# A table of due slots for side work in a three-phase attention kernel: the second phase's normalisation and post block put earlier, and more room ahead of a few steps

## Chip, cores and metric

One core of a Trainium2 chip runs the whole program. The metric is the device time of one execution in microseconds. The kernel is written in Bass with the order on every engine fixed when the program is built, and each engine works through its own list in order.

## What is computed

The input `x` has 32 sequences of 56 tokens with 160 features; `ctx_768` has 1500 context rows of 96 features for each sequence. Four blocks follow one another:

- L0: three short attentions (16 tokens each) against parts of the context, a weighted sum, output projection and residual.
- L1: layer norm, self attention (20 heads of 64), then cross attention over all 1500 context rows, then a gated feed-forward.
- L2: cross attention over 1496 context rows with 8 heads of 20, plus a small two-step attention over the 4 last context rows.
- L3: like L1 with 20 heads of 8.

Cut to its core, a long cross attention is:

```python
q = layer_norm(x) @ wq          # per head
scores = q @ (ctx @ wk).T * scale
out = softmax(scores) @ (ctx @ wv)
x = out @ wo + bo + x
```

## The kernel before

**Phases and pairs.** The program has three phases: phase 0 does L0 and L1, phase 1 (the "second phase" here) does L2, phase 2 does L3. A phase takes the 32 sequences as 16 pairs. For each pair and each half `b` of it (one sequence) the function `main` on TensorE runs the long cross attention: the context is cut into 12 chunks of 125 rows, and the heads into groups of at most 8 (8, 8 and 4 heads in phases 0 and 2; one group of 8 in phase 1). One chunk and group is a tile. It takes three matmuls into `ps_s` for the scores (L1133 to L1135), two exponentials on ScalarE (L1825 to `p32`, L1827 to `p_hi`), a subtraction on GpSimd (L1614, `p_lo`) and three matmuls into `ps_u` for the output (L1148 to L1150), three tiles behind the scores. "A group" below means three matmuls of one such set, 448 columns wide.

**Slots.** `main` counts slots: tile n has its scores at slot 2n and the outputs of tile n-3 at slot 2n+1. So one half is 24 slots long in phase 1, and 72 in phases 0 and 2.

**Side work.** Everything else is woven between the slots: `pre` (the short attentions and norms of the next pair), `context` (transposing the context, L1058, L1783, L1432), `queries` (L695 into `ps_c`, L1760, L1762, L1410), `maxima` (matmuls L1076 and the reductions L1455 and L1458 on VectorE, then `mneg` L1463, a transpose L1081 and `q_hi` L1468, without which the next half's scores can't begin), `post` (the projection L1094 of the attention's result, and in phases 0 and 2 the feed-forward), `hand` (L1495). Each is a generator that yields step numbers. The table `PARTS` gives for each part and phase a tuple (number of steps, weight, {step: extra room ahead of it}); `lane` lays a list of parts over the slots of one half, from `start` to the half's length less `tail`, and scales them to fit; `weave` runs main's slots and the lanes in order of slot. Room in `PARTS` is therefore relative: what one step gets is taken from the others of its lane. The same function runs on every engine.

**Normalisation.** At the end of a half, ScalarE copies the result out of `ps_u` into `uT` (L1815, at slot 6 of the next half in phase 1). Row 96 of it holds the sums. SyncE stores them (L623), loads them spread over partitions into `srec` (L626), VectorE takes the reciprocal (L1479) at slot `RECIP`, SyncE stores them (L629) and loads them broadcast to all partitions (L639, into `w_area` in phases 1 and 2), and VectorE multiplies `uT` by them (L1485) at slot `POST - 1`. `post` may start at slot `POST` in phase 1; it waits for that product. VectorE's list is strictly in order: while the reciprocal or the product waits for its transfer, the maxima behind it wait too.

```python
RECIP = 13
POST = 20
...
if t.ph == 1:
    weave(main(t, 0, first=first), lane(parts), lane(end, POST), *norm)
```

In phase 1, `parts` are `split`, `context(t, 1)` and `maxima(t, 1)`, and `end` is `post` of the pair before, `hand`, and the first 9 steps of `pre` of the next pair. In phase 1 these first steps are: take x (L1195 `x_mid`, L742, L745), the csT copy (L1334), L923 and L926, `pT` (L1338), L933, the masked keys `kvb` (L1340, L1260, L1344), the short scores L941, their maximum and difference (L1223, L1225), the exponential (L1651) and L763. So they are a chain between TensorE, VectorE and ScalarE.

## Time and profile before

| | us |
|---|---|
| median of 3 executions (lowest, highest) | 5963.16 (5962.99, 5965.48) |
| the profiled execution's own time | 5963.19 |
| span in the profile, first to last instruction | 5961.4 |
| TensorE matmul busy | 5579.6 (94%) |
| TensorE weight load busy | 4580.3 (77%) |
| VectorE, ScalarE, GpSimd busy | 2818.5, 3101.7, 3095.7 |
| mean granted TensorE clock | 0.961 of full |

The table's last line is the share of the full clock that was granted to TensorE over the span; windows of the trace give it stretch by stretch. TensorE's idle time comes with the instruction that ended it. All waits quoted are in microseconds unless marked ns.

### The profile page before, as it was taken

How to read it: one execution, taken by the hardware profiler on the slowest of the kernel's cores; microseconds unless marked ns; L12 is line 12 of the kernel's file. 1: busy time of each engine (PE TensorE's matmuls, PEld its weight loads, DVE VectorE, ACT ScalarE, POOL GpSimd, SP SyncE). 2: the span in 40 equal slices, each digit the busy share in tenths (PEclk: the TensorE clock that was granted, in tenths of full speed). 3: DMA queues.
4: the chain of work that ended last, by engine and by line, in shares of the span. 5: the costliest groups of instructions: out<-in, count | busy, mean ns of one | idle time of the engine just before them, and what ended most of it. 6: DMA issues, size and time to landing. Idle time of an engine off the chain costs nothing.

```text
span 5961.4 us, 92283 instructions
## 1 busy us (share of the span) xinstructions
PE 5579.6 (94%) x34224; PEld 4580.3 (77%) x34224; DVE 2818.5 (47%) x5171; ACT 3101.7 (52%) x7280; POOL 3095.7 (52%) x3472
## 2 busy tenths in 40 slices
PE   7999999999999999998989999799999999999998
PEld 5777777777777777786767767578888888888887
DVE  2444444444444444443555555255445455545452
ACT  1455555555554555553544544356566656566655
POOL 0445454444544445462555545256666666666665
PEclk8899999999999999997999989689999999999999
DMA  2000000000000000000111111100000000000000
GB/s 56 13 17 17 14 17 17 17 16 17 17 10 17 12 17 17 17 21 15 31 29 29 31 26 29 25 17 24 17 17 20 17 21 20 20 17 20 17 21 12
DMA packets 85964, 119.97 MB, mean 20 GB/s; under 512 B 42814, under 2 KB 65194, under 8 KB 85514
## 3 DMA queue, kind: packets, MB, share of 16 engines
q1 hardware_dynamic: 85514, 114.07, 6.9%
q8 instruction: 271, 4.44, 0.3%
q14 instruction: 179, 1.47, 0.1%
HBM read 109.56 MB, written 4.46 MB: 19 GB/s over the span
## 4 chain that ended last, share of the span: by engine, by line
PE 64%; DVE 18%; ACT 9%; DMA 3%; POOL 3%; issue 3%; ACTq 0%; POOLq 0%; SPq 0%; DVEq 0%
PE ps_c L695 13%; DVE mpiece L1458 8%; PE ps_s L1133 6%; PE ps_s L1134 5%; PE ps_s L1135 5%; PE ps_u L1148 5%; PE ps_c L1076 5%; PE ps_u L1150 4%; PE ps_u L1149 4%; PE ps_c L1094 3%; ACT p_hi L1827 2%; ACT p L1825 2%; POOL p_lo L1614 2%; DVE ctx_hi L1449 2%; DVE uT L1485 2%
## 5 line engine op out<-in xcount | busy, mean ns | idle before, releaser
L1614 POOL TENSOR_TENSOR p_lo<-p,p_hi 125x448 fp32r<-125x448 f32 (+2 forms) x2688 | 2716.5, 1019 | 2320.8 <-ACT p_hi L1827 1652.9
L1825 ACT ACTIVATE p<-ps_s 125x448 f32<-125x448 f32 (+2 forms) x2688 | 1324.7, 493 | 1822.6 <-PE ps_s L1135 1617.5
L1827 ACT ACTIVATE p_hi<-ps_s 125x448 fp32r<-125x448 f32 (+2 forms) x2688 | 1319.1, 491 | 0.0
L1458 DVE TENSOR_REDUCE mpiece<-ps_c 125x1 f32<-125x500 f32 (+1 forms) x1984 | 1226.8, 666 | 92.9 <-PE ps_c L1076 89.8
L1133 PE MATMUL ps_s<-q_hi,ctxT_hi 105*125 105x448 f32 (+3 forms) x2688 | 1005.0, 374 | 51.6 <-DVE q_hi L1468 28.5
L1148 PE MATMUL ps_u<-p_hi,ctx_hi 125*97 125x448 f32 (+2 forms) x2688 | 961.6, 358 | 16.1 <-ACT uT L1815 15.1
L1134 PE MATMUL ps_s<-q_lo,ctxT_hi 96*125 96x448 f32 (+2 forms) x2688 | 926.0, 345 | 0.0
L1135 PE MATMUL ps_s<-q_hi,ctxT_lo 96*125 96x448 f32 (+2 forms) x2688 | 922.0, 343 | 0.0
L1149 PE MATMUL ps_u<-p_hi,ctx_lo 125*96 125x448 f32 (+2 forms) x2688 | 914.7, 340 | 0.0
L1150 PE MATMUL ps_u<-p_lo,ctx_hi 125*97 125x448 f32 (+2 forms) x2688 | 913.8, 340 | 0.0
L1076 PE MATMUL ps_c<-ctxT_hi,q_hi 96*125 96x500 f32 (+1 forms) x2112 | 845.3, 425 | 67.5 <-DVE mpiece L1458 58.5
L1133 PEld LDWEIGHTS ps_s<-q_hi,ctxT_hi 105*125 105x125 f32 (+2 forms) x2688 | 507.1, 189 | 201.9 <-ACT p_hi L1827 55.3
L1076 PEld LDWEIGHTS ps_c<-ctxT_hi,q_hi 96*125 96x125 f32 (+1 forms) x2112 | 394.6, 188 | 254.5 <-DVE mpiece L1458 183.3
L1134 PEld LDWEIGHTS ps_s<-q_lo,ctxT_hi 96*125 96x125 f32 (+1 forms) x2688 | 513.1, 191 | 47.7
L1135 PEld LDWEIGHTS ps_s<-q_hi,ctxT_lo 96*125 96x125 f32 (+1 forms) x2688 | 513.0, 191 | 35.9
L1149 PEld LDWEIGHTS ps_u<-p_hi,ctx_lo 125*96 125x96 f32 (+1 forms) x2688 | 444.3, 165 | 91.7
L1150 PEld LDWEIGHTS ps_u<-p_lo,ctx_hi 125*97 125x97 f32 (+1 forms) x2688 | 440.3, 164 | 83.1
L1148 PEld LDWEIGHTS ps_u<-p_hi,ctx_hi 125*97 125x97 f32 (+1 forms) x2688 | 443.2, 165 | 59.6 <-issue 23.7
L1593 POOL TENSOR_TENSOR ctx_lo<-ctx_raw,ctx_hi 125x192 fp32r<-125x192 f32 x576 | 330.1, 582 | 184.7 <-DVE ctx_hi L1449 184.7
L695 PE MATMUL ps_c<-hT,w_m 80*96 80x112 f32 x3072 | 329.0, 268 | 33.1 <-ACT hT L1644 30.3
L695 PEld LDWEIGHTS ps_c<-hT,w_m 80*96 80x96 f32 x3072 | 318.3, 170 | 51.0 <-issue 43.7
L1410 DVE TENSOR_TENSOR q_lo<-ps_c,q_hi 96x224 fp32r<-96x224 f32 x192 | 74.4, 388 | 475.1 <-ACT q_hi L1762 475.1
(226 smaller groups left out, 5898.4 us busy)
## 6 DMA issues: line engine op xcount, KB each, us to landing
ctx_raw<-in_ctx SPq DMA_DIRECT2D x96, 562.5 KB
pT<-recs SPq DMA_DIRECT2D x32, 490.0 KB, 3.6
w_area<-recs SPq DMA_DIRECT2D x32, 490.0 KB, 3.6
w_area<-recs SPq DMA_DIRECT2D x32, 196.0 KB, 3.9
cs<-in_ctx SPq DMA_DIRECT2D x192, 6.0 KB, 3.2
x_between<-x_out SPq DMA_DIRECT2D x32, 80.0 KB
x_in<-x_between SPq DMA_DIRECT2D x32, 80.0 KB
w_area<-in_L_xattn_wq SPq DMA_DIRECT2D x2, 800.0 KB, 6.0
```

The costliest lines, as they stand in the source:

```text
L695: z = mm(dst, lhsT(i), rhs(i), start=(first and i == 0), stop=(last and i == 1))
L1076: mm(C(0, wide, n % banks(t), 0, PIECE), q_hi[0:DC, b, wide * k:wide * k + wide], ctxT_hi[0:DC, b, PIECE * r:PIECE * r + PIECE], start=Tru ...
L1133: mm(dst, ctxT_hi[0:rows_, b, k], q_hi[0:rows_, b, q], start=True, stop=False)
L1134: mm(dst, ctxT_hi[0:DC, b, k], q_lo[:, b, q], start=False, stop=False)
L1135: mm(dst, ctxT_lo[:, b, k], q_hi[0:DC, b, q], start=False, stop=True).then_inc(*sig("sc_psum"))
L1148: mm(dst, ctx_hi[0:kp, cb, c, :], p_hi[0:kp, k % RING, 0:w], start=(c == 0), stop=False)
L1149: mm(ps_u[0:DC, g, 0:w], ctx_lo[0:kp, cb, c, :], p_hi[0:kp, k % RING, 0:w], start=False, stop=False)
L1150: mm(dst, ctx_hi[0:kp, cb, c, :], p_lo[0:kp, k % 3, 0:w], start=False, stop=(c == NC - 1)).then_inc(*sig("pv_done"))
L1458: z = V.tensor_reduce(mpiece[0:wide, k, r:r + 1], C(0, wide, n % banks(t), 0, PIECE), AX.X, ALU.max)
L1614: P.tensor_tensor(p_lo[0:kp, k % 3, 0:w], p32[0:kp, k % 2, 0:w], p_hi[0:kp, k % RING, 0:w].bitcast(F32), ALU.subtract).then_inc(*sig("pl_r ...
L1825: A(p32[0:kp, k % 2, 0:w], ps_s[0:kp, k % 2, 0:w], ACT.Exp, scale=DH[t.ph] ** -0.5)
L1827: A(p_hi[0:kp, k % RING, 0:w], ps_s[0:kp, k % 2, 0:w], ACT.Exp, scale=DH[t.ph] ** -0.5)\
```

## The change

Numbers alone change in the table: nine entries of extra room grow (in `pre` steps 8, 27, 30, 35 of phase 0, step 5 of phase 1 and step 7 of phase 2; `queries` step 1 in phases 0 and 2; `post` step 6 in phase 0). For phase 1, `RECIP` goes from 13 to 10 and `POST` from 20 to 16, the lane with the maxima of the first half ends three slots earlier, and phase 2's first `pre` starts at slot 20 of phase 1's last half, before at 26 (behind the last score).

```diff
-            "pre": ((40, 3, {4: 1, 7: 0.5, 8: 3, 10: 1.5, 14: 1.5, 16: 3, 18: 2, 22: 2, 27: 2.5, 30: 1.5, 34: 1, 35: 0.5, 37: 1,
-                             38: 1.5, 39: 2, 40: 4.5}), (29, 3.5, {5: 2, 15: 1.5, 22: 0.5, 23: 2}), (20, 2.5, {2: 3, 6: 1.5, 7: 0.5, 9: 2, 11: 0.5, 13: 1, 15: 1, 19: 2, 20: 1})),
-            "queries": ((7, 1, {1: 2, 7: 3}), (3, 3, {1: 1}), (7, 1, {1: 2, 7: 2})),
+            "pre": ((40, 3, {4: 1, 7: 0.5, 8: 4, 10: 1.5, 14: 1.5, 16: 3, 18: 2, 22: 2, 27: 3, 30: 2, 34: 1, 35: 1.5, 37: 1,
+                             38: 1.5, 39: 2, 40: 4.5}), (29, 3.5, {5: 2.5, 15: 1.5, 22: 0.5, 23: 2}), (20, 2.5, {2: 3, 6: 1.5, 7: 1.2, 9: 2, 11: 0.5, 13: 1, 15: 1, 19: 2, 20: 1})),
+            "queries": ((7, 1, {1: 5, 7: 3}), (3, 3, {1: 1}), (7, 1, {1: 5, 7: 2})),
...
-            "post": ((15, 3, {1: 1, 6: 1, 14: 1}), (2, 1.5, {1: 1}), (15, 3, {1: 0.5, 6: 1.5})),
+            "post": ((15, 3, {1: 1, 6: 2, 14: 1}), (2, 1.5, {1: 1}), (15, 3, {1: 0.5, 6: 1.5})),
...
-        RECIP = 13
-        POST = 20
+        RECIP = (13, 10, 13)
+        POST = (20, 16, 20)
...
-                    weave(main(t, 0, first=first), lane(parts), lane(end, POST), *norm)
+                    weave(main(t, 0, first=first), lane(parts, 0.0, TAIL - 1), lane(end, POST[1]), *norm)
...
-                    lanes = [lane([part("pre", side.pre, At(t.ph + 1, 0, ahead=True))], POST + 6.0)]
+                    lanes = [lane([part("pre", side.pre, At(t.ph + 1, 0, ahead=True))], POST[t.ph] + (4.0 if t.ph else 6.0))]
```

(`normalise` reads `RECIP[t.ph]` and `POST[t.ph]` now.)

How this moves instructions is seen at two places of a steady pair of phase 1. First VectorE in the pair's first half, from the last context piece to the product: before,

```order
L1458 TENSOR_REDUCE mpiece<-ps_c 112x1
L1449 CAST ctx_hi<-ctx_raw 125x4x96
L1458 TENSOR_REDUCE mpiece<-ps_c 112x1
L1455 TENSOR_REDUCE mpiece<-ps_c 112x1
L1479 RECIPROCAL srec<-srec 112x4
L1449 CAST ctx_hi<-ctx_raw 125x4x96
L1458 TENSOR_REDUCE mpiece<-ps_c 112x1 x2
L1449 CAST ctx_hi<-ctx_raw 125x4x96
L1455 TENSOR_REDUCE mpiece<-ps_c 112x1
L1458 TENSOR_REDUCE mpiece<-ps_c 112x1 x2
L1455 TENSOR_REDUCE mpiece<-ps_c 112x1
L1485 TENSOR_TENSOR uT<-uT,w_area 97x8x56
```

and now:

```order
L1479 RECIPROCAL srec<-srec 112x4
L1458 TENSOR_REDUCE mpiece<-ps_c 112x1
L1449 CAST ctx_hi<-ctx_raw 125x4x96
L1458 TENSOR_REDUCE mpiece<-ps_c 112x1
L1455 TENSOR_REDUCE mpiece<-ps_c 112x1
L1449 CAST ctx_hi<-ctx_raw 125x4x96
L1458 TENSOR_REDUCE mpiece<-ps_c 112x1 x2
L1449 CAST ctx_hi<-ctx_raw 125x4x96
L1455 TENSOR_REDUCE mpiece<-ps_c 112x1
L1458 TENSOR_REDUCE mpiece<-ps_c 112x1
L1485 TENSOR_TENSOR uT<-uT,w_area 97x8x56
```

The reciprocal now stands ahead of the first reduction instead of behind the third, and the product behind the seventh of the twelve instead of behind the ninth.

Second TensorE near the end of the same half, from L933 to the short scores L941 and the transposed maxima L1081: before,

```order
L933 MATMUL ps_u<-pT,w_s 80x128 x2
L1133 MATMUL ps_s<-q_hi,ctxT_hi 124x448
L1134 MATMUL ps_s<-q_lo,ctxT_hi 124x448
L1135 MATMUL ps_s<-q_hi,ctxT_lo 124x448
L1148 MATMUL ps_u<-p_hi,ctx_hi 97x448
L1149 MATMUL ps_u<-p_hi,ctx_lo 96x448
L1150 MATMUL ps_u<-p_lo,ctx_hi 97x448
L941 MATMUL ps_u<-kvb,qo 64x256 x4
L1081 MATMUL ps_c<-ident,mneg 4x112
```

and now:

```order
L933 MATMUL ps_u<-pT,w_s 80x128 x2
L1133 MATMUL ps_s<-q_hi,ctxT_hi 124x448
L1134 MATMUL ps_s<-q_lo,ctxT_hi 124x448
L1135 MATMUL ps_s<-q_hi,ctxT_lo 124x448
L1081 MATMUL ps_c<-ident,mneg 4x112
L1148 MATMUL ps_u<-p_hi,ctx_hi 97x448
L1149 MATMUL ps_u<-p_hi,ctx_lo 96x448
L1150 MATMUL ps_u<-p_lo,ctx_hi 97x448
L1133 MATMUL ps_s<-q_hi,ctxT_hi 124x448
L1134 MATMUL ps_s<-q_lo,ctxT_hi 124x448
L1135 MATMUL ps_s<-q_hi,ctxT_lo 124x448
L941 MATMUL ps_u<-kvb,qo 64x256 x4
```

The transposed maxima come ahead of the short scores, and one group more stands in front of the latter. Over the whole stretch from L1094 to L763 TensorE had four groups woven in before and has eight now; the four that were added stood ahead of L1094 before. In phases 0 and 2 single groups change places with a side step: in phase 0 one group now stands ahead of L763, one ahead of the queries' L695, and L1094 comes one group earlier while L1101 stays; in phase 2 one more group stands ahead of the queries' L695, and ScalarE has the `hT` it waits for (L1644) one pair of exponentials earlier.

## Rows read from the trace of the kernel before

**Rows 1.** The page, busy time: us (share of the span), instructions.

```profile
PE 5579.6 (94%) x34224; PEld 4580.3 (77%) x34224; DVE 2818.5 (47%) x5171; ACT 3101.7 (52%) x7280; POOL 3095.7 (52%) x3472
```

**Rows 2.** Windows: length, busy PE PEld DVE ACT POOL, PEclk, DMA, GB/s.

```profile
2794.00:3683.40 889.40, 814.80 (x4595) 624.90 (x4592) 500.50 (x996) 443.56 (x980) 485.64 (x506) 0.93 0.13 29
...
3049.20:3109.50 60.30, 54.73 (x329) 42.05 (x328) 36.02 (x71) 31.63 (x70) 34.65 (x36) 1.00 0.13 28
...
3235.30:3300.10 64.80, 59.89 (x328) 45.94 (x328) 35.35 (x72) 31.72 (x70) 34.41 (x36) 0.89 0.11 29
3365.60:3426.60 61.00, 55.91 (x328) 43.32 (x328) 35.08 (x71) 31.61 (x70) 34.43 (x36) 0.97 0.13 28
...
219.10:2469.40 2250.30, 2144.91 (x13812) 1775.57 (x13813) 1022.73 (x1821) 1162.01 (x2710) 1105.17 (x1264) 1.00 0.05 16
3945.20:5744.60 1799.40, 1746.79 (x11154) 1482.43 (x11153) 919.79 (x1667) 1087.51 (x2607) 1119.03 (x1262) 1.00 0.06 19
```

**Rows 3.** Windows, phase 1: a pair's time at half clock.

```profile
3175.80:3189.50 13.70, 12.05 (x53) 8.95 (x54) 3.71 (x8) 4.07 (x8) 3.07 (x3) 0.50 0.01 2
```

**Rows 4.** Timeline, PE, one pair (start, length, instruction, [idle before it, ended by]).

```profile
3106.38 2.44 PE L1094 MATMUL ps_u<-w_n,uT 96*128 96x160 f32 x16 [0.47 <-DVE uT L1485]
...
3114.84 1.09 PE L941 MATMUL ps_u<-kvb,qo 80*64 80x256 f32 x8 [0.74 <-DVE kvb L1344]
...
3117.96 0.73 PE L1133 MATMUL ps_s<-q_hi,ctxT_hi 100*125 100x448 f32 x1 [1.75 <-DVE q_hi L1468]
...
3119.24 1.05 PE L763 MATMUL ps_c<-ident,sm 128*128 128x128 f32 x4
```

**Rows 5.** Timeline, DVE and ACT, the same pair.

```profile
3097.18 0.68 DVE L1458 TENSOR_REDUCE mpiece<-ps_c 112x1 f32<-112x500 f32 x1 [0.78 <-PE ps_c L1076]
...
3104.73 1.59 DVE L1485 TENSOR_TENSOR uT<-uT,w_area 97x448 f32<-97x448 f32 x1 [0.41 <-DMA w_area<-recs]
...
3111.68 0.28 DVE L1338 COPY pT<-ps_u 4x128 f32<-4x128 f32 x1 [0.50 <-PE ps_c L926]
...
3114.61 0.15 DVE L1463 TENSOR_REDUCE mneg<-mpiece 112x4 f32<-112x12 f32 x1
...
3117.28 0.58 ACT L1651 ACTIVATE sm<-sm 128x448 f32<-128x448 f32 x1 [2.78 <-DVE sm L1225]
```

**Rows 6.** Timeline, SyncE's queue, the same pair; then DMA issues, phase 1, to landing.

```profile
3095.39 0.32 SPq L626 DMA_DIRECT2D srec<-sums  x1
3099.42 0.31 SPq L629 DMA_DIRECT2D recs<-srec  x1
3100.81 0.30 SPq L639 DMA_DIRECT2D w_area<-recs  x1
...
w_area<-recs SPq DMA_DIRECT2D x25, 196.0 KB, 3.9
...
srec<-sums SPq DMA_DIRECT2D x25, 1.8 KB, 1.6
```

**Rows 7.** PE's waits, phase 0, 14 pairs (total, times, longest).

```profile
PE ps_c L1076 <- DVE mpiece L1458: 28.4, 44, 1.0
PE ps_c L695 <- ACT hT L1644: 13.1, 14, 0.9
PE ps_c L763 <- DVE sm L1241: 12.9, 13, 1.0
PE ps_c L1101 <- DVE xn L1521: 9.6, 14, 0.7
```

**Rows 8.** PE's waits, phase 2, 14 pairs.

```profile
PE ps_c L695 <- ACT hT L1644: 14.5, 15, 1.0
```

**Rows 9.** Timeline, PE, the end of phase 1's last half.

```profile
3765.86 0.36 PE L1148 MATMUL ps_u<-p_hi,ctx_hi 124*97 124x448 f32 x1
...
3766.47 0.36 PE L1148 MATMUL ps_u<-p_hi,ctx_hi 124*97 124x448 f32 x1
...
3771.06 0.62 PE L755 MATMUL ps_c<-ident,xn 128*80 128x128 f32 x2 [3.82 <-DVE xn L1216]
```

More of the change, by code:

```diff
@@ L1476, in normalise @@
                     tiles = t.heads // 2
-                    yield RECIP
+                    yield RECIP[t.ph]
                     dve.wait_ge(*got("su_loaded", t, 16 * (b + 1)))
@@ L1480, in normalise @@
                     for g, (h0, n) in enumerate(t.groups):
-                        yield POST - 1 + (APART[t.ph] if b else 2) * g
+                        yield POST[t.ph] - 1 + (APART[t.ph] if b else 2) * g
                         if g == 0:
```

## Prediction

> **What bounds the kernel.** I read four views, from wide to narrow. The page says that TensorE is busy 94% of the span and every other engine about half [rows 1], so the path is TensorE's list, and time can only come from its idle time, or from its clock. The windows view tells the phases apart [rows 2]: the 14 steady pairs of phase 0 take 160.7 us each (2250.3 / 14) with 7.5 us idle, those of phase 2 128.5 us (1799.4 / 14) with 3.8 us idle, both at a granted clock of 1.00. The 14 pairs of phase 1 take 63.5 us each (889.4 / 14) at a mean clock of 0.93. The clock has two levels, so 0.93 means 889.4 x 0.07 x 2 = 125 us at 1.2 GHz, the rest at 2.4. Single pairs show what that costs: one at 1.00 throughout takes 60.3 us, one at 0.97 (3.7 us low) 61.0, one at 0.89 (14.3 us low) 64.8. All 14 lie 889.4 - 14 x 60.3 = 45 us above the pair that never fell. So phase 1 loses 45 us to the clock, 0.36 us for each us low; it is below a half since part of the low time is spent waiting anyway.
>
> **Where the clock falls** [rows 3, 4]. The 12.9 us from the projection L1094 (3106.38) to L763 (3119.24) hold only four groups of full matmuls and a chain of small ones; TensorE waits for the product (0.47), for `kvb` ahead of L941 (0.74), and for `q_hi` ahead of the next scores (1.75). In another pair the 13.7 us from 3175.8 on run at 0.50, and they begin where such a chain has just passed. That stretch is what the change takes apart.
>
> **Phase 1, full clock.** The chain of transfers first. `srec` is issued at 3095.39 and takes 1.6, so the sums are there at 3097.0; the first reduction starts at 3097.18 [rows 5, 6]. The reciprocal, now ahead of it, waits for nearly nothing. What it does cost: the first maxima matmuls come a group earlier, and VectorE doesn't follow. From L629, which follows the reciprocal, to the issue of the broadcast pass 1.4 us (3099.42 to 3100.81), and it takes 3.9 to land; with 0.2 for the reciprocal a start at 3097.0 gives 3102.5. The product today starts at 3104.73 after 0.41 of waiting; two reductions of 0.6 less stand ahead of it now, so VectorE is there at 3103.0: the transfer has landed by 0.5 us. L1094 can then start at about 3104 where it started at 3106.38. But it stands four groups earlier, and one group lasts 0.61 (3765.86 to 3766.47, [rows 9]): 2.4 us of work is only moved behind it. There it meets the chain again. `mneg` comes 2.93 us after `pT` starts (3114.61 less 3111.68, [rows 5]), while only L933 and one group (together 1.2 us) stand between them on TensorE now: I get 1.4 us of waiting at L1081. The exponential ends 3.0 us after L941 starts (3117.86 less 3114.84, [rows 4, 5]), and L941 itself (1.0) and two groups (1.2) cover 2.2: 0.8 us at L763. `x_mid` adds some 0.8, since a reduction now stands ahead of its copy, and the denser maxima 1.0 to 1.5. That is 4 to 4.5 us of waits in place of 3.8 today (0.47, 0.74, 1.75 and three of 0.2 to 0.4). **So at full clock I expect no gain: a pair stays at 60.3, between -1.0 (the waits at L1094 and L1081 vanish) and +1.5 (reciprocal or product miss their transfers).**
>
> **Phase 1, clock.** The gain is that the same idle time is spread. Between L1094 and L763 there are eight groups for four, and TensorE's longest stretch without a full group shrinks from L941, L1081 and 1.75 of waiting (some 3.2 us) to 1.4 + 0.3. Nearest rows for the price: the pair that never fell, 60.3, and the one at 0.89, 64.8 [rows 2]. I take that a third of the low time is left, since one wait of 1.4 us beside L933 still looks like what stands there now. That is 8.9 us (125 / 14) down to 3, times 0.36: 2.1 us a pair; less 0.3 for the waits above, 1.8. Times 15 pairs (the last has no such stretch): **-27 us**; ends 0 and 15 x 3.2 = -48. The Trainium skill ("TensorE: Matmul & The Clock Gate", Terms) puts the penalty at throttled time x (1 - K/N), a half of it. By that phase 1 would lose 62 us, not the 45 that the rows show, and the term would be -43; the rows decide.
>
> **Phase 0** [rows 7]. Three waits come once a pair: L763 for `sm` 1.0, the queries' L695 for `hT` 0.94, L1101 for `xn` 0.7. Each now has one group more ahead of it: 0.61 each, 1.8 in all. Against it the first block of 27 maxima matmuls has 19 groups among it for 20, and the wait on `mpiece` is already 2.0 a pair (28.4 / 14): +0.3. Net -1.5, times 15 pairs: **-22 us**. Ends: -5 (the time is only handed to `mpiece`) and -28 (no such loss). The other steps with more room (27, 30, 35) move no group past a side step, and cost and bring nothing.
>
> **Phase 2** [rows 8]. The one wait is L695 for `hT`, 1.0 us; one group more stands ahead and ScalarE has it earlier, so it goes: **-14 us**. Ends -5 and -15. Next late there is `mpiece`, whose density doesn't change.
>
> **Handover to phase 2** [rows 9]. Putting its first `pre` at slot 20 saves little: L755 waits 3.82 for `xn`, which stands on VectorE behind a product that waits for its own transfer, in both kernels. Three groups now fall into waits that are there anyway: **-2 us**, between 0 and -5.
>
> The sum is 5963.2 (the profiled execution, which is the median of the runs too) - 27 - 22 - 14 - 2 = **5898 us**. About 0.2%, 12 us, is what a measurement of this kernel tells from no change.
>
> **Rivals.**
>
> - *The clock no longer falls.* For it: the pair at 1.00 has the same instructions as its neighbours [rows 2], so the present stretch is near the edge, and any filling may do. Against: waits of 1.4 and 0.8 remain. 5963 - 48 - 38 = 5877.
> - *It falls as often as now.* For it: the sum of waits doesn't shrink. Then only phases 0 and 2 count: 5963 - 38 = 5925.
> - *Room is only handed on.* Every wait covered turns up as a wait for `mpiece`, and the clock stays: 5961.
> - *Slower: small waits over a longer stretch.* The waits reach from the first dense maxima (3098 in that pair's time) to L763, some 20 us for 12.9 now. If TensorE's clock falls at the first of them and stays low to the end, 20 us low x 0.36 gives 67.5 us a pair, 4.0 more than the mean now: 5963 + 60 - 38 = 5985. It decides once a pair spends over 16 us low: 15 x 0.36 x (16 - 8.9) is the 38 us gained elsewhere. For it: the falls now last up to 14 us once begun [rows 3]. Against: groups stand between the new waits. The Trainium skill ("TensorE: Matmul & The Clock Gate", A second HAM failure mode) tells of a kernel whose clock swings because TensorE idles briefly and often between groups of matmuls; by that rule spreading the waits would be the wrong way. The trace doesn't bear it out so far: the maxima stretches of phase 0 have such short waits, and hold 1.00.
>
> **Chances.** The forecast 0.45, no more falls 0.22, falls as now 0.17, room handed on 0.09, slower 0.07. Faster by over 0.2% is the first three, 0.84; within it 0.09; slower 0.07. The range must reach over the first three with the ends of phases 0 and 2: down to 5877 less 6 + 1 + 3 and the full-clock gain of about 5, so 5862; up to 5925 plus some 27 where phases 0 and 2 give only their small ends (17 + 9): 5952.
>
> **What would show it.** Phase 1's pairs at 60 to 62 us with a mean clock of 0.97 or more; a wait of 1 to 1.5 us at L1081 for `mneg` and 0.8 at L763 for `sm`, none at L941; `q_hi` gone from the scores' waits; VectorE's product without a wait for `w_area` in the first half. In phase 0 the waits of L763, L695 and L1101 down by 0.6 each, in phase 2 that of L695 gone. I am wrong if phase 1's clock stays at 0.93, if the product waits over 1 us for its transfer, or if `mpiece` rises by over 1 us a pair.

## Result and profile after

The changed kernel takes **5938.77 us** (median of 9 runs, 5931.98 to 5952.63) against 5964.34 for the kernel before in the same series (9 runs, 5953.14 to 5967.7): ratio 0.9964, 95% interval 0.9953 to 0.9974. That is 25.6 us faster where I forecast 65. Sign and range held, the size didn't.

The page's busy time, after:

```profile
PE 5570.6 (94%) x34224; PEld 4568.5 (77%) x34224; DVE 2827.2 (48%) x5171; ACT 3092.0 (52%) x7280; POOL 3117.8 (53%) x3472
```

TensorE has the same 34224 instructions and is busy 9.0 us less [rows 1]: the same work at a higher clock. The windows view of the changed kernel (length, busy PE PEld DVE ACT POOL, PEclk, DMA, GB/s): phase 0, phase 1, phase 2, the two pairs at the handover, then two single pairs of phase 1.

```profile
218.70:2468.20 2249.50, 2138.84 (x13813) 1778.58 (x13813) 1032.47 (x1820) 1155.27 (x2710) 1105.16 (x1264) 1.00 0.05 16
2787.90:3657.90 870.00, 803.29 (x4598) 601.63 (x4596) 488.78 (x997) 443.18 (x982) 509.70 (x509) 0.96 0.12 29
3923.90:5718.10 1794.20, 1750.25 (x11153) 1489.91 (x11152) 930.72 (x1667) 1087.21 (x2607) 1114.91 (x1262) 1.00 0.06 19
2788.00:2848.80 60.80, 56.40 (x334) 42.28 (x332) 35.52 (x73) 32.31 (x72) 38.98 (x41) 1.00 0.12 31
2848.80:2912.70 63.90, 59.79 (x328) 44.45 (x328) 34.60 (x72) 31.64 (x70) 36.24 (x37) 0.92 0.12 28
3657.90:3923.90 266.00, 228.43 (x1094) 170.59 (x1095) 107.55 (x202) 95.33 (x231) 91.86 (x99) 0.71 0.10 23
```

Against [rows 2], by stretch of the two profiled executions (a stretch begins where the pair's x is taken; low is time at 1.2 GHz, added up from the clock's records):

| stretch | before us (low) | after us (low) | difference |
|---|---|---|---|
| start and first pair | 219.1 (71.7) | 218.7 (71.7) | -0.4 |
| phase 0, 14 pairs | 2250.3 (20.5) | 2249.5 (6.8) | -0.8 |
| the two pairs between phases 0 and 1 | 324.6 (81.9) | 319.7 (75.1) | -4.9 |
| phase 1, 14 pairs | 889.3 (122.9) | 870.0 (64.9) | -19.3 |
| the two pairs between phases 1 and 2 | 261.9 (143.4) | 266.0 (153.6) | +4.1 |
| phase 2, 14 pairs | 1799.3 (0) | 1794.2 (17.1) | -5.1 |
| the rest | 216.8 (27.6) | 218.9 (34.5) | +2.1 |
| span | 5961.4 | 5937.0 | -24.4 |

Phase 1 brings most, and by the clock: 58 us less low time at the prediction's 0.36 are 21 us. The quickest pair that never falls takes 60.2 (the only such pair before took 60.3). The times of single runs say the same: of the nine, the fastest (5931.98) had a mean clock of 0.967, the slowest (5952.63) 0.962.

**Phase 1's waits.** TensorE's timeline in one pair (start, length, instruction, [idle before it, ended by]), to be laid beside [rows 4]:

```profile
3092.46 0.45 PE L1076 MATMUL ps_c<-ctxT_hi,q_hi 96*112 96x500 f32 x1 [0.67 <-DVE mpiece L1458]
...
3099.26 0.48 PE L1076 MATMUL ps_c<-ctxT_hi,q_hi 96*112 96x500 f32 x1 [1.13 <-DVE mpiece L1458]
3099.58 2.33 PE L1094 MATMUL ps_u<-w_n,uT 96*128 96x160 f32 x16
...
3103.34 0.41 PE L745 MATMUL ps_u<-ident,x_mid 128*80 128x128 f32 x2 [0.48 <-DVE x_mid L1195]
...
3108.68 0.35 PE L1081 MATMUL ps_c<-ident,mneg 112*4 112x112 f32 x2 [1.15 <-DVE mneg L1463]
...
3110.36 1.09 PE L941 MATMUL ps_u<-kvb,qo 80*64 80x256 f32 x8
...
3113.54 0.63 PE L763 MATMUL ps_c<-ident,sm 128*128 128x128 f32 x4 [0.68 <-ACT sm L1651]
```

VectorE's timeline there (compare [rows 5]):

```profile
3091.57 0.18 DVE L1479 RECIPROCAL srec<-srec 112x4 f32<-112x4 f32 x1 [1.22 <-DMA srec<-sums]
...
3097.00 1.61 DVE L1485 TENSOR_TENSOR uT<-uT,w_area 97x448 f32<-97x448 f32 x1 [0.27 <-DMA w_area<-recs]
```

This is the pair of the 14 with the longest waits for `mpiece` ahead of L1094 (0.67 and 1.13; in most pairs there is none there). So the sums over the 14 pairs say more (total, times, longest). Before:

```profile
PE ps_s L1133 <- DVE q_hi L1468: 22.5, 14, 1.8
...
PE ps_u L941 <- DVE kvb L1344: 10.9, 14, 1.2
PE ps_c L1076 <- DVE mpiece L1458: 9.8, 14, 0.7
PE ps_u L1094 <- DVE uT L1485: 5.0, 8, 1.6
```

After:

```profile
PE ps_c L1076 <- DVE mpiece L1458: 21.4, 34, 1.1
PE ps_c L1081 <- DVE mneg L1463: 16.0, 14, 1.2
...
PE ps_u L745 <- DVE x_mid L1195: 7.1, 14, 1.1
PE ps_c L763 <- ACT sm L1651: 3.8, 6, 0.7
```

The waits for the product, `kvb` and `q_hi` are gone, and those that I had worked out stand in their place. From L1094 to L763 it is now 14.0 us for 12.9, with more groups between.

**Phase 0.** TensorE's waits over 14 pairs (total, times, longest):

```profile
PE ps_c L1076 <- DVE mpiece L1458: 39.1, 57, 2.4
PE ps_s L1133 <- ACT p_hi L1827: 11.9, 27, 0.6
PE ps_c L1094 <- DVE q_hi L1468: 9.7, 14, 0.7
...
PE ps_c L755 <- DVE xn L1216: 6.8, 13, 0.5
PE ps_c L695 <- ACT hT L1644: 4.6, 14, 0.3
```

L763's wait for `sm` (12.9 in [rows 7]) and L1101's for `xn` (9.6) have left the list, and `hT` is down from 13.1 to 4.6. But `mpiece` is up by 10.7, the scores now wait 11.9 for `p_hi` (3.7 before), and L1094 waits 9.7 for `q_hi`, which it didn't before. The idle time of the 14 pairs is 110.7 us for 105.4: the room was handed on. What did go is low time, 6.8 us for 20.5. Before, the clock falls for 3.4 us in 6 of the 14 pairs, each time 126 to 130 us into the pair, among the maxima matmuls. L1076 has then just waited 0.6 and 1.0 us for `mpiece`, in all six. One of them (windows view of the kernel before, as above):

```profile
501.00:509.90 8.90, 7.18 (x35) 5.21 (x34) 8.90 (x16) 3.17 (x8) 8.07 (x12) 1.00 0.18 57
509.90:513.30 3.40, 3.40 (x11) 2.71 (x10) 3.01 (x6) 0.98 (x2) 1.14 (x1) 0.51 0.31 98
```

After, the second of these waits is 0.16 us, another of 0.8 stands 10 us behind it, and no pair falls at this place.

**Handover.** TensorE's timeline, to [rows 9]:

```profile
3746.58 0.62 PE L755 MATMUL ps_c<-ident,xn 128*80 128x128 f32 x2 [3.92 <-DVE xn L1216]
...
3795.45 4.58 PE L1094 MATMUL ps_u<-w_n,uT 96*128 96x160 f32 x16 [10.07 <-DVE uT L1485]
```

### The profile page after: what moved, and what is told of

It is laid out like the page before. It is cut to its first block, busy times and chain, and to the rows that moved or that the text cites. A ratio compares the mean times of both kernels' runs of the same rounds, so it can differ in the third digit from the quotient of the medians.

```text
span 5937.0 us, 92283 instructions
## 1 busy us (share of the span) xinstructions
PE 5570.6 (94%) x34224; PEld 4568.5 (77%) x34224; DVE 2827.2 (48%) x5171; ACT 3092.0 (52%) x7280; POOL 3117.8 (53%) x3472
## 4 chain that ended last, share of the span: by engine, by line
PE 64%; DVE 21%; ACT 8%; DMA 3%; issue 3%; POOL 2%; ACTq 0%; POOLq 0%; SPq 0%; DVEq 0%
PE ps_c L695 14%; DVE mpiece L1458 9%; PE ps_s L1133 6%; PE ps_u L1148 5%; PE ps_s L1134 5%; PE ps_s L1135 5%; PE ps_u L1150 4%; PE ps_u L1149 4%; PE ps_c L1076 4%; PE ps_c L1094 3%; DVE ctx_hi L1449 2%; ACT p_hi L1827 2%; DVE uT L1485 2%; ACT p L1825 2%; POOL p_lo L1614 1%
## 5 line engine op out<-in xcount | busy, mean ns | idle before, releaser
L1076 PE MATMUL ps_c<-ctxT_hi,q_hi 96*125 96x500 f32 (+1 forms) x2112 | 846.2, 425 | 106.1 <-DVE mpiece L1458 87.6
L1076 PEld LDWEIGHTS ps_c<-ctxT_hi,q_hi 96*125 96x125 f32 (+1 forms) x2112 | 393.5, 187 | 305.4 <-DVE mpiece L1458 220.3
L1593 POOL TENSOR_TENSOR ctx_lo<-ctx_raw,ctx_hi 125x192 fp32r<-125x192 f32 x576 | 343.5, 606 | 204.8 <-DVE ctx_hi L1449 203.6
L695 PE MATMUL ps_c<-hT,w_m 80*96 80x112 f32 x3072 | 328.4, 268 | 8.7 <-ACT hT L1644 5.9
L695 PEld LDWEIGHTS ps_c<-hT,w_m 80*96 80x96 f32 x3072 | 318.8, 170 | 21.3 <-issue 14.3
```

The lines of the kernel that those rows point to most:

```text
L695: z = mm(dst, lhsT(i), rhs(i), start=(first and i == 0), stop=(last and i == 1))
L1076: mm(C(0, wide, n % banks(t), 0, PIECE), q_hi[0:DC, b, wide * k:wide * k + wide], ctxT_hi[0:DC, b, PIECE * r:PIECE * r + PIECE], start=Tru ...
```

## Experiments

Each ratio is to the kernel before, run on the same chip. "Phase 1" below is the length of its 14 pairs in the profiled execution, with the low time behind it.

### The change in two halves

`a1_phase1_only` is the changed kernel with the rooms of phases 0 and 2 back, as in the diff. `a2_others_only` is the kernel before with the rooms of phases 0 and 2 at the change's values; phase 1's table entries, slots, lane and handover are left as they were.

```diff
-            "pre": ((40, 3, {4: 1, 7: 0.5, 8: 4, 10: 1.5, 14: 1.5, 16: 3, 18: 2, 22: 2, 27: 3, 30: 2, 34: 1, 35: 1.5, 37: 1,
-                             38: 1.5, 39: 2, 40: 4.5}), (29, 3.5, {5: 2.5, 15: 1.5, 22: 0.5, 23: 2}), (20, 2.5, {2: 3, 6: 1.5, 7: 1.2, 9: 2, 11: 0.5, 13: 1, 15: 1, 19: 2, 20: 1})),
-            "queries": ((7, 1, {1: 5, 7: 3}), (3, 3, {1: 1}), (7, 1, {1: 5, 7: 2})),
+            "pre": ((40, 3, {4: 1, 7: 0.5, 8: 3, 10: 1.5, 14: 1.5, 16: 3, 18: 2, 22: 2, 27: 2.5, 30: 1.5, 34: 1, 35: 0.5, 37: 1,
+                             38: 1.5, 39: 2, 40: 4.5}), (29, 3.5, {5: 2.5, 15: 1.5, 22: 0.5, 23: 2}), (20, 2.5, {2: 3, 6: 1.5, 7: 0.5, 9: 2, 11: 0.5, 13: 1, 15: 1, 19: 2, 20: 1})),
+            "queries": ((7, 1, {1: 2, 7: 3}), (3, 3, {1: 1}), (7, 1, {1: 2, 7: 2})),
...
-            "post": ((15, 3, {1: 1, 6: 2, 14: 1}), (2, 1.5, {1: 1}), (15, 3, {1: 0.5, 6: 1.5})),
+            "post": ((15, 3, {1: 1, 6: 1, 14: 1}), (2, 1.5, {1: 1}), (15, 3, {1: 0.5, 6: 1.5})),
```

> The change without its table entries for phases 0 and 2 (phase 1's slots, lane, pre step 5 and the handover stay). Theory, from the windows of the two traces: nearly the whole gain is phase 1's, where the 14 steady pairs went from 889.4 to 870.0 us; phases 0 and 2 keep 160.7 and 128.5 us a pair; so 5964 - 19 for phase 1, + 4 for the handover, or about 5945 to 5950. Rival, my forecast of before: the entries for phases 0 and 2 are worth 1.5 and 1.0 us a pair, and this kernel stays some 35 us slower than the full change would with them.

> The table entries for phases 0 and 2 alone, phase 1 as before. Theory (the waits are handed on): 160.1 us a pair of phase 0 with idle time of 6.8 us, the wait at L763 turning up as 0.6 at the scores just ahead of it and that at L1101 as 0.7 at L1094; phase 2 at 126.9 us where the clock holds and 1.5 more where it falls; in all 5 to 12 us faster than before, 5952 to 5959. Rival (the covers count in full, phase 0 lost elsewhere): over 20 us faster, below 5944. A third reading, that phase 2's new falls of the clock come from phase 1 or from chance, would show none here.

Measured: a1 5951.48 us, 0.9973 (0.9962 to 0.9983); a2 5957.51 us, 0.9988 (0.9979 to 0.9997). Both halves gain, 14 and 8 us of the 26. a1 lies 1.5 us above its theory's 5945 to 5950, far from the rival's 35 us behind the full change. a2 lies in its theory's range: the waits are handed on, and phase 2's falls are there (13.7 us low) though phase 1 is the old one. Phase 1 of a1 took 893.8 us (119.5 low), though its code there is that of the changed kernel:

```profile
2778.67:3672.49 893.82, 826.49 (x4598) 616.76 (x4596) 490.55 (x997) 443.52 (x982) 510.30 (x509) 0.93 0.12 29
```

So one profile doesn't size phase 1. The same phase 1 code was profiled five times (changed kernel, a1, a3, a4, d2): 870.0 (64.9), 893.8 (119.5), 878.0 (71.7), 881.5 (92.2), 874.7 (58.0). The mean is 879.6 us at 81 us low; the 870.0 of the result is the best of five. In a2, phase 0 with the new rooms takes 2246.9 us and phase 2 1790.9. Its phase 1 has the order of the kernel before on TensorE, VectorE and ScalarE, instruction for instruction, and took 898.2 us (153.6 low):

```profile
2788.55:3686.77 898.22, 826.51 (x4594) 633.67 (x4592) 496.69 (x996) 444.17 (x980) 485.96 (x506) 0.91 0.13 29
```

So the old phase 1 has two profiles, 889.3 and 898.2, mean 893.8 us at 138 us low. By the means phase 1 gained 14 us, which is also what a1 gained in all. And the 25 pairs without a fall in the five profiles took 60.2 to 61.9 us, 60.8 in the mean, where the only one in the two old profiles took 60.3. Most are of two sorts: L1076's wait of 1.1 us for `mpiece` just ahead of L1094 is there in those of some 61.3 us and missing in those of 60.2.

### Is it the clock?

`b1_after_filler` and `b2_before_filler` put three more products of 448 columns ahead of one tile's scores, a little ahead of the chain, in the first halves of phase 1. The scores overwrite them, so the output is unchanged.

```diff
 # scores(n), TensorE; b1: the changed kernel, n == 10; b2: the kernel before, n == 11
+for _ in range(3 if t.ph == 1 and b == 0 and n == 10 else 0):
+    mm(dst, ctxT_hi[0:rows_, b, k], q_hi[0:rows_, b, q], start=True, stop=True)
 mm(dst, ctxT_hi[0:rows_, b, k], q_hi[0:rows_, b, q], start=True, stop=False)
```

> The changed kernel, with the first score matmul of the eleventh tile done three times more in each first half of phase 1 (same operands and target, overwritten by the real one; 0.6 us of full matmuls ahead of L1081's wait of 1.15 us). Theory (the clock falls for want of work in that stretch): the wait at L1081 shrinks to 0.5, the falls of 6.8 to 10.2 us vanish in most pairs, and phase 1's pairs go from 62.1 to 60.2 us, so 15 to 25 us faster than the change, 5915 to 5925, with more work. Rival (the falls are not set by this stretch, but by chance or by the waits in the maxima): the low time stays at about 65 us over 14 pairs, and the time at 5939 or a few us above.

> The kernel before, with the first score matmul of the twelfth tile done three times more in each first half of phase 1 (overwritten by the real one; 0.6 us ahead of L941's wait of 0.74 us). Theory (the clock): the falls that begin at L941 go, those that begin after it (11 us behind L1094, L941 itself and 1.75 us of waiting) stay; low time from 123 us over 14 pairs to 60 to 90, the time 8 to 15 us below before, 5949 to 5956. Rival (work added is work paid): 14 x 0.1 to 0.6 us slower and the same low time, 5964 to 5972.

Measured: b1 5914.72 us, 0.9914 (0.99 to 0.9927); b2 5935.61 us, 0.9947 (0.9936 to 0.9959). The windows view of b1, phase 1:

```profile
2791.41:3643.22 851.81, 784.29 (x4640) 591.31 (x4638) 491.45 (x996) 442.45 (x982) 509.65 (x509) 1.00 0.12 30
```

42 products more and 19.0 us less busy time than the changed kernel: no low time is left (64.9 there), and idle time is as it was (67.5 us for 66.7). A pair takes 60.8 us in the mean, as the changed kernel's pairs without a fall do: L1081's wait is 0.57 us for 1.15, so the products stand in a wait. b2 has 47.8 us low for 122.9 and takes 860.5, a gain twice what its theory had (5949 to 5956); b1's 5915 to 5925 held to within 0.3 us. More work made both kernels faster, by 24 and 30 us, so what phase 1 loses against pairs of 60.8 us is lost to the clock. `e1_filler_one` has one such product for three.

> The changed kernel with one overwritten product of 448 columns, for three, ahead of the scores of tile 10 in the first halves of phase 1. Theory A (the chain of waits and narrow products is just over the edge, as the pairs that don't fall show, so 0.2 us of full work is nearly enough): low clock in the 14 pairs 0 to 25 us, the stretch 846 to 858 us, the time 5910 to 5920 us. Rival B (it takes the 0.6 us of three): low clock 35 to 60 us, the stretch 860 to 868 us, the time 5925 to 5937.

Measured: 5927.27 us, 0.9934 (0.9922 to 0.9947), phase 1 871.0 us (58.0 low). The low time and the time are rival B's, the stretch a little over it: one isn't enough.

### Handover and phase 2

`a3_old_handover` starts phase 2's first `pre` at slot 26 again (`POST[t.ph] + 10.0` for `+ 4.0`).

> The changed kernel with the steps ahead of phase 2 started at slot 26 again, as before the change, instead of slot 20. Theory A (the earlier start thins out the end of the last pair of phase 1, so that the clock stays low for longer): the two pairs at the handover take 261 to 263 us as before instead of 266, low clock 143 us instead of 154, and the whole is 2 to 5 us shorter than the changed kernel. Rival B (those 4 us are scatter from one execution to the next): the stretch stays at 265 to 267 us with 150 us or more of low clock, or moves the time by less than 1 us. In either the rest of the program reads as in the changed kernel.

Measured: 5936.38 us, 0.9944 (0.993 to 0.9958); the two pairs took 263.5 us (143.4 low). That reads as theory A has it, but other kernels say that it is rival B's scatter: a1, d2 and e1 start at slot 20 as the changed kernel does and took 263.1, 262.8 and 264.0 us (143 to 150 low), and a2, which starts at slot 26, took 265.4 (157.0). The times don't tell them apart either: the intervals of after and a3 overlap. No effect of the handover's slot shows.

`a4_ph2_step7_back` has phase 2's `pre` step 7 at `7: 0.5`, `d2_ph2_queries_back` has phase 2's queries at `(7, 1, {1: 2, 7: 2})`.

> The changed kernel with the room ahead of step 7 of phase 2's pre block at 0.5 again instead of 1.2. Theory A (the step moved ahead of the 40 short L772 products leaves a stretch with one group of wide products fewer, in which the clock falls): the falls of 3.4 us at about +50 us of phase 2's pairs go (14 to 17 us of low clock in the 14 pairs to 0) and the hT wait of 1.0 us is back in each pair, so that the 14 pairs take 1793 to 1799 us against 1794. Rival B (the falls come from the earlier handover or from the clock's history): they stay with 14 us or more, and the pairs are 1 us longer each, 1805 us or more.

> The changed kernel with the room of phase 2's queries at 2 again instead of 5; step 7 of its pre block stays at 1.2. In the run with step 7 back the 3.4 us falls of phase 2 stayed (20 us) and the wait for hT stayed away, while L1007 waited 0.6 us a pair more for the kept products. Theory A (the queries' room covers the wait for hT and brings the falls; step 7's room covers the wait at L1007 alone): the wait for hT is back at 14 us over 14 pairs, the falls are gone (0 to 3 us), and the 14 pairs take 1792 to 1800 us against 1794. Rival B (any earlier step ahead of the short products lets the clock fall): falls of 14 us or more stay and the 14 pairs take 1802 us or more.

Measured: a4 5954.36 us, 0.9966 (0.9953 to 0.998); d2 5958.31 us, 0.9988 (0.9979 to 0.9997). TensorE's waits in phase 2, changed kernel:

```profile
PE ps_c L1076 <- DVE mpiece L1458: 19.4, 42, 1.0
...
PE ps_c L1007 <- DVE vb_s L1260: 5.5, 14, 0.4
```

a4:

```profile
PE ps_c L1007 <- DVE vb_s L1260: 13.9, 14, 1.0
```

d2:

```profile
PE ps_c L695 <- ACT hT L1644: 11.4, 15, 0.8
```

The queries' room covers the wait for `hT` (0.2 us left in a4 and after); step 7's keeps L1007's wait from growing by 0.6 a pair. Phase 2 took 1799.3 us with neither, 1802.1 (20.5 low) with the queries' room alone, 1809.4 (17.1) with step 7's alone, 1794.2 (17.1) with both. In the whole time a4 (0.9966) can't be told from the changed kernel (0.9964), while d2 is 0.24% slower, 14 us: of the two edits the queries' room is the one that shows. On the falls of 3.4 us there theory A fell both times; they come with either edit, as rival B had it for d2 (and for a4, but for its 1805 us). They aren't in every execution either: e1, with both edits, had 3.4 us low and took 1785.3. Over the nine kernels that have both edits phase 2 took 1785.3 to 1795.9 us at 3.4 to 20.5 us low, 1791 in the mean, against 1798.3 to 1800.1 at 0 to 3.4 in the five with neither. From the ends of that row I estimate 0.6 us for a low us here.

### Phase 1: early slots or shorter lane?

`b3_lane_only` is the kernel before with the lane three slots shorter; `d4_long_lane` the changed kernel with it long; `f1_late_post` the changed kernel with the slots late; `f2_early_post_only` the kernel before with the slots early; `f3_shorter_lane` takes two slots more off the lane.

```diff
 b3, against the kernel before (d4 has `lane(parts)` in the changed kernel)
-                    weave(main(t, 0, first=first), lane(parts), lane(end, POST), *norm)
+                    weave(main(t, 0, first=first), lane(parts, 0.0, TAIL - 1), lane(end, POST), *norm)
 f3, against the changed kernel
-                    weave(main(t, 0, first=first), lane(parts, 0.0, TAIL - 1), lane(end, POST[1]), *norm)
+                    weave(main(t, 0, first=first), lane(parts, 0.0, TAIL + 1), lane(end, POST[1]), *norm)
 f1, against the changed kernel (f2 has the early values in the kernel before)
-        RECIP = (13, 10, 13)
-        POST = (20, 16, 20)
+        RECIP = (13, 13, 13)
+        POST = (20, 20, 20)
```

> The kernel before with one edit: phase 1's maxima lane three slots shorter. It takes away the wait of 1.75 us for q_hi at the first scores of the second half and leaves reciprocals, products and post block at their late slots, next to the maxima. Theory A (falls hang on how many waits and narrow products stand close together after the post block): the lane brings the maxima closer to the post block, low clock in the 14 pairs of phase 1 stays at 110 to 150 us and the stretch takes 885 to 895 us. Rival B (the q_hi wait alone makes the clock fall): low clock falls to 65 us or less and the stretch to 872 us or less, with the time at 5945 us.

> The changed kernel with phase 1's maxima lane at its full length again; reciprocals, products and post block stay at slots 10 to 16. Theory A (most of what the change gains in phase 1 comes from the space between the post block and the second half's first scores, the lane adds the q_hi wait of 1.75 us back as a second place to fall): low clock in the 14 pairs 80 to 120 us, the stretch 878 to 890 us, the time 5945 to 5955. Rival B (the lane does nothing once the post block stands early): 65 to 92 us of low clock and 870 to 882 us, as in the three executions of the changed phase 1, time 5936 to 5945. Rival C (the lane is the whole gain: alone it brought 12 us of the 19): 115 us or more and 889 us or more.

> The changed kernel with phase 1's reciprocals, products and post block at slots 13 to 20 again; the short maxima lane and all room elsewhere stay, the handover starts at slot 20 as in the change. Theory A (the lane is phase 1's whole gain, and the early slots bring nothing in themselves): phase 1's 14 pairs 870 to 885 us with 50 to 90 us of low clock, as with the early slots, the time 5935 to 5948 us. Rival B (the early slots and the lane only work together, since the one takes the other's new waits away): the stretch 885 us or more and the time 5950 us or more. Rival C (the early slots now even cost, by the waits at L1081 and L763): the stretch 865 us or less, the time below 5932.

> The kernel before with one edit: phase 1's reciprocals, products and post block at slots 10 to 16. Lane, rooms and handover stay. Theory A (the early slots bring nothing in themselves): the 14 pairs of phase 1 take 885 to 898 us with 100 to 155 us of low clock, as in the kernel before, the time 5960 to 5972 us. Rival B (my forecast's term, by spreading the small work alone): low clock at 90 us or less, the stretch at 875 us or less, the time 5945 to 5953.

> The changed kernel with phase 1's maxima lane two slots shorter still. Theory A (the lane gains by the space between the last maxima with mneg and the second half's scores, and that wait is gone already): nothing more to gain, the denser maxima wait for their pieces, the pair that never falls rises from 60.2 to 60.6 to 61.2 us, phase 1's 14 pairs take 876 to 892 us, the time 5940 to 5955. Rival B (more distance, fewer falls): low clock 50 us or less, the stretch 866 us or less, the time 5934 or less.

| | lane | slots | us | ratio (interval) | phase 1 (low) | pair that never falls |
|---|---|---|---|---|---|---|
| before, first series | long | late | 5964.34 | 1 | 889.3 (122.9), in a2 898.2 (153.6) | 60.3 |
| f2 | long | early | 5969.73 | 1.0007 (0.9995 to 1.0018) | 897.8 (102.4) | 60.6 |
| d4, all else changed | long | early | 5960.17 | 0.999 (0.9981 to 0.9998) | 894.2 (105.8) | 60.6 |
| b3 | short | late | 5952.94 | 0.9974 (0.9964 to 0.9985) | 877.7 (51.2) | 61.1 |
| f1, all else changed | short | late | 5948.1 | 0.997 (0.9959 to 0.9981) | 878.2 (54.6) | 61.1 |
| after | short | early | 5938.77 | 0.9964 (0.9953 to 0.9974) | mean of five 879.6 (81) | 60.2 to 61.9, mean 60.8 |
| f3, all else changed | shorter | early | 5928.7 | 0.9941 (0.9928 to 0.9954) | 863.5 (10.2) | 61.2 |

The early slots, the part of the change that I had put phase 1's gain on, bring nothing with the long lane (f2; and d4 is no faster than a2, which hasn't them). The lane alone brings 0.26% of the time, 15 us, and as much again with the early slots (d4 against after); in phase 1 it is 16 us by the means of two profiles each (before and a2; b3 and f1, whose order in phase 1 is the same). With the short lane the early slots lower the pair without a fall from 61.1 to 60.8 in the mean and raise the low time from about 53 to 81 us; in the stretch that cancels (878 against 880). In the time f1 and after differ by 0.06%, less than their intervals. So theory A for f2, theory A for f1 (its time is on the upper edge) and, by the stretch alone, rival C for d4 are what the numbers fit. b3 lies between its two theories: falls are rarer (5 pairs of 14) than A said, and the stretch longer than B said.

Why the early slots need the lane shows in VectorE's product, all 28 of phase 1 (busy, mean ns | idle before them). Before:

```profile
L1485 DVE TENSOR_TENSOR uT<-uT,w_area 97x448 f32<-97x448 f32 x28 | 27.0, 965 | 11.9 <-DMA w_area<-recs 11.7
```

f2, early slots with the long lane:

```profile
L1485 DVE TENSOR_TENSOR uT<-uT,w_area 97x448 f32<-97x448 f32 x28 | 26.8, 958 | 23.2 <-DMA w_area<-recs 23.2
```

After, early slots with the short lane:

```profile
L1485 DVE TENSOR_TENSOR uT<-uT,w_area 97x448 f32<-97x448 f32 x28 | 24.8, 886 | 2.2 <-DMA w_area<-recs 1.6
```

In the first half of a pair 6 reductions stand between reciprocal and product before, 5 in f2, 7 after and 8 in b3. Five don't cover the broadcast's flight (3.9 us to landing, [rows 6]). VectorE stands 23.2 us, and TensorE, over 14 pairs of f2, waits in turn:

```profile
PE ps_c L1076 <- DVE mpiece L1458: 36.8, 43, 1.6
PE ps_u L1094 <- DVE uT L1485: 15.8, 14, 1.9
...
PE ps_s L1133 <- DVE q_hi L1468: 12.0, 14, 1.0
```

In b3, late slots with the short lane, the waits are these:

```profile
PE ps_c L763 <- ACT sm L1651: 17.1, 14, 1.3
...
PE ps_u L941 <- DVE kvb L1344: 10.9, 14, 1.2
PE ps_c L1076 <- DVE mpiece L1458: 9.8, 14, 0.7
PE ps_c L1081 <- DVE mneg L1463: 7.7, 14, 0.6
```

and in f3:

```profile
PE ps_c L1076 <- DVE mpiece L1458: 32.5, 42, 2.6
PE ps_u L745 <- DVE x_mid L1195: 19.9, 14, 1.5
...
PE ps_c L763 <- ACT sm L1651: 9.4, 14, 0.7
```

f3 is the telling one. TensorE idles 84.6 us in phase 1, as long as in f2 (84.7; before 74.6, after 66.7), a pair without a fall takes 61.2 us for 60.8, and yet the kernel is faster than the changed one: its phase 1 is shorter than in any of the five profiles of the changed code, and the intervals of the two ratios only touch. In its timeline L1081 stands between the small matmuls of `pre`, seven us ahead of L763, with no wait of its own:

```profile
3101.22 0.35 PE L1081 MATMUL ps_c<-ident,mneg 112*4 112x112 f32 x2
...
3108.27 0.63 PE L763 MATMUL ps_c<-ident,sm 128*128 128x128 f32 x4 [0.69 <-ACT sm L1651]
```

The windows view of its phase 1:

```profile
2788.81:3652.28 863.47, 778.88 (x4595) 586.31 (x4595) 504.02 (x996) 441.59 (x982) 511.23 (x506) 0.99 0.12 30
```

I had expected f3 to be slower; rival B held. So the sum of the waits doesn't decide. That what decides is whether the waits and the small matmuls stand close together at the end of the half fits b3 and f3, but no run here moved them apart at the same sum; it stays my reading.

### A faster version

`c1_all_fillers` and `d3_best` are b1 with more overwritten products at the ends of the phases. c1 also has step 7 of phase 2 at 0.5; d3 starts the handover at slot 26.

```diff
 post(t, last), TensorE, c1; d3 has range(9)
                     yield 1
+                    if last:
+                        pe.wait_ge(*got("exp_done", t, 2 * NC * len(t.groups)))
+                        for _ in range(28):
+                            mm(ps_s[0:128, 0, 0:480], w_n[0:96, 0, 0:128], w_n[0:96, 0:3, :], start=True, stop=True)
                     pe.wait_ge(*got("ut_ready", t, 2))
 scores(n), TensorE, c1, in place of b1's loop; d3 has 11: 4
+                    for _ in range(3 if t.ph == 1 and b == 0 and n == 10 else {10: 20, 11: 8}.get(n, 0) if t.ph == 1 and last else 0):
```

> The changed kernel with step 7 of phase 2 back, 3 overwritten products ahead of tile 10's scores in the first halves of phase 1 as in the run before, and more overwritten products at the ends of the phases: 20 and 8 ahead of the last two score tiles of phase 1, and 28 wide ones of 480 columns ahead of the last post block of each phase, where TensorE waits 10 us for the products. The output is not changed. Theory A (the 154 us of low clock at the handover begin because TensorE stands still for 5.3, 2.4, 2.5, 3.2 and 10 us there, and each us of it costs 0.37 us): the handover's two pairs drop from 264 to 235 us or less at 70 us of low clock or less, the first pair of phase 1 from 320 to 300 us, and the whole takes 5860 to 5890 us. Rival B (the low clock there lasts because of the narrow products and waits of the stretch itself, 80 short products of w_m and w_area, whatever ran before): low clock stays above 110 us, the handover at 258 us or more, and the time at 5905 to 5915 us as with the 3 products alone.

> The version that the runs point to: the changed kernel with the handover's start at slot 26, three overwritten products ahead of tile 10 in the first halves of phase 1, 20 and 4 ahead of the last two score tiles of phase 1, and 9 wide ones (0.85 us each by the run with 28, so 7.6 us) ahead of the last post block of each phase, inside its wait of 10 us. Against the run with three products alone the one with 28 was 13 us too long at each of three places (23.8 us in a wait of 10) and gained 4 to 9 us beside that at each. Theory A (what it gained there stays when the excess goes): handover 250 to 257 us, phase 1's first two pairs 315 to 319, last stretch 210 to 214, the whole 5893 to 5903 us. Rival B (nine products end too long before the narrow work for the clock to hold): each of the three stretches as with three products alone, 262 to 264, 320 to 322 and 217, the whole 5910 to 5915 us.

Measured: c1 5946.59 us, 0.9961 (0.9949 to 0.9974); d3 5912.35 us, 0.9909 (0.9896 to 0.9922). c1's 28 products took 23.8 us in a wait of 10: my sizing, by a price I hadn't measured. Against b1 the three ends took 22 us more, and phase 2, with step 7 back, 7.5. Theory A fell; of rival B the handover held (112.6 us low, 268.3 us), the time didn't. d3 lies where rival B put it. Its handover took 265.3 us with 126.3 low, b1's 263.8 with 143.4: low time went, and the products cost what it gave. So d3 and b1 are equal, 0.9% faster than the kernel before: 0.4 by the change and 0.5 by the three products in phase 1.

## Why the prediction was wrong in size

**Phase 1, clock: -27 forecast.** Two sentences failed: "The gain is that the same idle time is spread" and "I take that a third of the low time is left". The price per low us was right: (63.9 - 60.2) / 10.2 = 0.36 here too (in b3 it is 4.3 / 10.2 = 0.42). The amount wasn't: 65 us of low time are left of 123 in the profile, 81 in the mean of five. The 81 is three fifths of the 138 us that the old code has in the mean of its two. By the two profiled executions phase 1 gave 19 us, by the means 14: some 21 won on 57 us less low time, less 7 lost at full clock. And the cause was another. I had entered the shorter lane as a cost (denser maxima, 1.0 to 1.5 us) and the early slots as the gain; the runs show the lane as the gain (b3) and the early slots as nothing by themselves (f2). The replay of the waits was good and didn't help: 1.4 forecast at L1081 and 1.15 found, 0.8 and 0.68 at L763 (in the pairs without a fall), 0.8 and 0.5 at L745, 1.0 to 1.5 more for the maxima and 0.8 more in the mean (21.4 for 9.8 over the 14), `kvb` and `q_hi` gone. The reciprocal was said to wait for nearly nothing; VectorE stands 0.6 us ahead of it in most pairs and 1.2 in the one shown. The pair was forecast at 60.3 and took 60.2 at best, 60.8 in the mean, so that the term at full clock, put at 0.3 us a pair, was 0.5. I had even said what remained against a rise of the clock ("waits of 1.4 and 0.8 remain"), and then took a third without a row. (The term of -43 that the prediction works out from the half price leaves out the 0.3 us a pair of its own sum; with it, it is -40.)

**Phase 0: -22 forecast, -0.8 found,** and some -2 over all kernels (2248.4 to 2250.3 in the five with the old rooms, 2246.3 to 2249.5 in all of those with the new but f1, 2253.0). The step that goes from "0.61 each, 1.8 in all" to +0.3 for `mpiece` against it failed on its second part: `mpiece` took 0.8 a pair, and `p_hi` ahead of the scores (0.6), `q_hi` ahead of L1094 (0.7) and `xn` at L755 (0.3) took the rest, 2.3 a pair for 2.2 won. The low time of phase 0 was 17 to 44 us with the old rooms and is 0 to 14 with the new, and that brought next to nothing: b2 and b3, with 17.1 and 44.4 us low, took 2250.3 and 2249.9. That is the rival "room is only handed on", to which I had given 0.09 and which I should have held for phase 0 alone.

**Phase 2: -14 forecast, -5.1 found.** The wait for `hT` went as said, 1.0 a pair. `mpiece` took 0.36 a pair of it, 5 us, though I had said that its density doesn't change. The rest went to new falls of the clock, which the prediction had put at nothing: with nearly none of them (e1, 3.4 us low) the stretch gave what I forecast, 1785.3 against 1799.3, 14.0; over the nine kernels it gave 8. How much each took stays open: by the 0.6 estimated above the 17.1 us low alone would be some 10.

**Handover: -2 forecast, +4.1 found,** by 10 us more low time; with slot 26 (a3) it is +1.6. As other kernels with slot 20 took 262.8 to 264.0 us, most of the +4.1 is scatter, and the -2 doesn't show.

**The slower rival** (small waits over a longer stretch) was wrong in the changed kernel. f2 is nearest to it: there low time begins again at L1094 or up to 2 us behind its start in five pairs, but its 897.8 us are no more than the old code's 898.2 in a2, so it isn't shown to be slower. What I had said against this rival, that phase 0's maxima stretches "hold 1.00", was a misreading of a rounded mean: 20.5 us there were low, in just those stretches. The Trainium skill ("TensorE: Matmul & The Clock Gate", A second HAM failure mode) describes brief idle times between groups of matmuls under which the clock swings; the falls beside waits of 0.6 to 1.9 us here, phase 0's among them, fit that, but by f3, which idles more and falls less, the sum of such waits doesn't tell how often.

## What to carry over

Where an engine's clock can fall, an edit has two prices, idle time and falls, and they may have opposite signs (f3: 18 us more idle, 10 us faster). A replay of waits from the trace gives the first; the second wants a measurement on several executions of both kernels, since the same code gave 870 to 894 us. And a low us hasn't one price: next to nothing in phase 0, where the falls stood among waits, 0.36 to 0.42 us in phase 1, some 0.6 in phase 2. And room taken inside one lane with full engines is handed on unless the wait that stands next to it is checked too: write down what is late next for each wait, not once for the sum.

## What I had not expected of the hardware

Three products of 448 columns whose results are thrown away, some 0.6 us at full clock in each of 16 pairs, make the kernel 24 to 30 us faster by keeping 1.2 GHz away (b1, b2). One of them does part of it (5927 us), and 28 wide ones in front of the phases' ends do little: the clock falls again in the narrow products that follow (low from 3794.8 to 3880.1 in c1). And how often the clock falls in the same code differs from one execution to the next by up to a factor of two, 58 to 120 us in five executions, while the idle time stays within 67 to 75 us; and the single runs of a kernel, 20 us apart, go with their mean clock.
